# A four-layer graph network on one core: edge destinations loaded one round further ahead, and degree products made in one bf16 pass

## The reference, cut to what matters

```python
deg = segment_sum(ones_like(dst), dst, num_segments=n)                # degrees
x = layernorm(x + gcn(x, W1, b1, W2, b2, edge_index))                 # 2 sums over neighbours
x = layernorm(x + gated(x, src, dst, ...))                            # 1 sum (in and out)
agg = segment_sum(edge_attr_64, dst, num_segments=n)                  # edge attributes
x = layernorm(x + mlp(concat([x, agg, u]), w1, w2, w3))
x = layernorm(x + sage(x, src, dst, ...))                             # 2 sums over neighbours
```

## Time and profile before

| | |
|---|---|
| runs of the kernel before | 833.84, 836.97 and 837.99 us, median 836.97 |
| the profiled execution's own time | 836.0 us |
| its span, first to last instruction | 834.3 us |
| PE, DVE, ACT busy, share of the span | 88%, 70%, 40% |
| rounds of the first part | from 26 us to 230 us |
| mean granted clock of TensorE | 0.934 of full speed |

### The profile page before, as it was taken

One profiled execution on the slowest core, in us unless ns is written; L12 is line 12 of the kernel. 1 busy time (PEld: TensorE's weight loads), 2 busy tenths in 40 slices (PEclk: granted clock), 3 DMA queues, 4 the chain that ended last, 5 costly groups with the idle time before them and its releaser, 6 DMA issues.

```text
span 834.3 us, 20354 instructions
## 1 busy us (share of the span) xinstructions
PE 731.2 (88%) x8590; PEld 651.4 (78%) x8590; DVE 586.0 (70%) x884; ACT 329.8 (40%) x587; POOL 25.5 (3%) x44
## 2 busy tenths in 40 slices
PE   5467878888869999999989998869979999999994
PEld 2367868887769999899989996535539998699994
DVE  6999999989847777787876773757566554045554
ACT  0464545554544322522463223264325232432233
POOL 4700000000000000000000000000000000000000
PEclk9788997987969999999989999989988999999997
DMA  5445766766422000000000000000000000000001
GB/s 137 115 127 158 209 189 187 202 183 184 127 38 58 1 1 1 2 1 1 1 22 1 1 1 3 1 13 1 0 1 26 0 0 1 0 1 1 1 25 53
DMA packets 48710, 43.28 MB, mean 52 GB/s; under 512 B 26370, under 2 KB 31141, under 8 KB 48549
## 3 DMA queue, kind: packets, MB, share of 16 engines
q1 hardware_dynamic: 36042, 39.81, 17.0%
q10 hardware_dynamic: 11932, 0.81, 1.0%
q0 software_dynamic: 640, 1.29, 0.6%
HBM read 39.08 MB, written 2.01 MB: 49 GB/s over the span
## 4 chain that ended last, share of the span: by engine, by line
PE 76%; DVE 13%; issue 6%; ACT 2%; DMA 1%; SPq 1%; ACTq 0%; DVEq 0%
PE bank L1781 21%; PE bank L1782 21%; PE bank L1693 5%; PE bank L1709 4%; PE bank L1697 3%; PE bank L1678 2%; PE bank L1989 2%; PE bank L1713 2%; PE bank L1997 2%; PE bank L1843 1%; DVE early L1101 1%; PE bank L2040 1%; PE bank L2041 1%; PE bank L1794 1%; PE bank L1856 1%
## 5 line engine op out<-in xcount | busy, mean ns | idle before, releaser
L1781 PE MATMUL bank<-stage,f_hi 125*128 125x392 f32 x1000 | 348.7, 349 | 2.2 <-issue 2.2
L1782 PE MATMUL bank<-stage,f_lo 125*128 125x392 f32 x1000 | 342.4, 342 | 0.0
L1181 DVE CAST stage<-counts 125x2352 fp32r<-125x2352 uint8 x120 | 164.3, 1380 | 80.4 <-PE bank L1782 80.2
L828 ACT ACTIVATE stage<-counts 125x1568 fp32r<-125x1568 uint8 x80 | 108.1, 1351 | 227.6 <-PE bank L1782 224.6
L1781 PEld LDWEIGHTS bank<-stage,f_hi 125*128 125x128 f32 x1000 | 189.9, 190 | 3.5 <-issue 2.4
L1782 PEld LDWEIGHTS bank<-stage,f_lo 125*128 125x128 f32 x1000 | 189.8, 190 | 0.6
L781 ACT ACTIVATE counts<-bank 125x500 uint8<-125x500 f32 (+1 forms) x157 | 81.6, 594 | 58.2 <-PE bank L1697 55.9
L1693 PE MATMUL bank<-early 128*128 128x125 bf16 x625 | 81.5, 250 | 25.6 <-issue 17.8
L1693 PEld LDWEIGHTS bank<-early 128*128 128x128 bf16 x625 | 71.6, 116 | 27.7 <-issue 27.7
L1101 DVE TENSOR_TENSOR early<-tmp 128x5000 bf16<-128x5000 bf16 (+1 forms) x32 | 86.3, 2696 | 0.0
L1697 PE MATMUL bank<-early 128*128 128x75 bf16 x625 | 80.9, 225 | 0.5 <-issue 0.5
(11 more groups left out here) (244 smaller groups left out, 822.2 us busy)
## 6 DMA issues: line engine op xcount, KB each, us to landing
wb<-in_edge_attr SPq DMA_DIRECT2D x95, 256.0 KB, 3.2
rowb<-in_edge_attr SPq DMA_DIRECT2D x30, 256.0 KB, 3.3
wa<-in_x SPq DMA_DIRECT2D x12, 125.0 KB
out<-wl SPq DMA_DIRECT2D x6, 250.0 KB
tmp<-in_dst SPq DMA_DIRECT2D x63, 4.0 KB, 3.0
tmp<-in_dst ACTq DMA_DIRECT2D x62, 4.0 KB, 2.8
eaT<-eaT SPq DMA_DIRECT2D x1, 784.0 KB, 5.8
wb<-in_L_gnn_w_ih SPq DMA_DIRECT2D x1, 384.0 KB, 3.5
```

Source lines behind the costliest of these rows:

```text
L828: nc.scalar.activation(set_buffer(u, m), counts[:, SETS[u][0]:sum(SETS[u]), chunk(c)], ACT.Copy).then_inc(s["set_a_ready"], 1)
L1181: nc.vector.tensor_copy(set_buffer(u, m), counts[:, SETS[u][0]:sum(SETS[u]), chunk(pair * 2 + off)]).then_inc(s["set_d_ready"], 1)
L1781: mm(bank[h][:, 0:CH], f_hi[:, first + k, :], rhs[:, k, :], start=(first + k == 0), stop=False)
L1782: last = mm(bank[h][:, 0:CH], f_lo[:, first + k, :], rhs[:, k, :], start=False, stop=(first + k == HI - 1))
```

## The change

Destinations get a ring of `RD = 12` slots, three rounds, with three semaphores instead of two. SP issues the destinations of even block e + 4 where it issued those of block e, behind the same wait for block e - 8; ACT issues the odd ones of three rounds ahead instead of two, and six instead of four before the first round. For that SP loads a second start into a register, once for each even block. DVE's wait counts three semaphores; nothing else changes on DVE.

The degree products take bf16 operands: as weights the upper 16 bits of each fp32 element of the one-hot (`upper[r][:, :, 1]`, exact for 0 and 1), a step of two bf16 elements, and a bf16 one (`one_bf`) instead of the fp32 one. The number of matmuls in the program stays 8 for each edge block.

```diff
@@ -50,6 +50,7 @@
 ECAP = TE * 128
 EB = 4
 RE = 2 * EB
+RD = 3 * EB
 EPP = E // LO
 GE = 33
 NG = E // GE
@@ -171,7 +172,7 @@
 
         iota_l = carve(128).bitcast(BF16).rearrange("p (l j) -> p l j", j=2)
         iota_w = wl1[:, 400:400 + EB * TE * EW].rearrange("p (j w) -> p j w", w=EW)
-        dst_e = carve(RE * TE).bitcast(I32).rearrange("p (r j) -> p r j", r=RE)
+        dst_e = carve(RD * TE).bitcast(I32).rearrange("p (r j) -> p r j", r=RD)
         starts_i = carve(NE + 1)[0:1, :].bitcast(I32)
         key_base = carve(NQ)
         past_block = carve(NQ)
@@ -179,7 +180,8 @@
         oh_last = carve(3 * 2 * HI).bitcast(BF16).rearrange("p (b m k j) -> p b m k j", m=2, k=HI, j=2)
         crowded = carve(NQ)
         list_idx = carve(NQ).bitcast(I32)
-        one_f = wb[:, 6 * TE * DE:6 * TE * DE + 1]
+        one_bf = wb[:, 6 * TE * DE:6 * TE * DE + 1].bitcast(BF16)[:, 0:1]
+        upper = [a[:, :].bitcast(BF16).rearrange("p (w h) -> p w h", h=2) for a in oh_dst_row]
         ea_in = [a[:, r * TE * DE:(r + 1) * TE * DE].rearrange("p (j f) -> p j f", j=TE)
                  for a, n in ((wb, 6), (rowb[:, 2 * nd:], RE - 6)) for r in range(n)]
 
@@ -246,7 +248,7 @@
         g_rows_in = {k: sem(f"g_rows_in{k}") for k in (0, 1, 2, 3, 5, 6, 7)}
         out_done = [sem(f"out_done{b}") for b in range(3)]
         list_in = [sem(f"list_in{q}") for q in range(NQ)]
-        dst_ready = [sem(f"dst_ready{r}") for r in range(2)]
+        dst_ready = [sem(f"dst_ready{r}") for r in range(3)]
         ea_ready = [sem(f"ea_ready{r}") for r in range(2)]
 
         def wait_stored(eng, k):
@@ -564,15 +566,21 @@
             sp.wait_ge(s["starts_made"], 1)
             sp.wait_ge(s["slots_clean"], 1)
 
-            for e in range(NE):
+            def destinations(e):
+
                 if e == QL // BW + 1:
                     sp.wait_ge(s["starts_made"], 2)
+                sp.dma_start(dst_e[:, e % RD, :], dst[bass.ds(sp.value_load(starts_i[0:1, e:e + 1]), ECAP)].rearrange("(p j) -> p j", j=TE)).then_inc(dst_ready[e // EB % 3], 16)
+
+            for e in range(0, EB, 2):
+                destinations(e)
+            for e in range(NE):
                 first = sp.value_load(starts_i[0:1, e:e + 1])
                 if e >= RE:
                     sp.wait_ge(s["ea_made"], e - RE + 1)
                 sp.dma_start(ea_in[e % RE], edge_attr[bass.ds(first, ECAP), :].rearrange("(p j) c -> p j c", j=TE)).then_inc(ea_ready[e // EB % 2], 16)
-                if e % 2 == 0:
-                    sp.dma_start(dst_e[:, e % RE, :], dst[bass.ds(first, ECAP)].rearrange("(p j) -> p j", j=TE)).then_inc(dst_ready[e // EB % 2], 16)
+                if e % 2 == 0 and e + EB < NE:
+                    destinations(e + EB)
                 if e >= X_FROM and (e - X_FROM) % X_EVERY == 0 and (e - X_FROM) // X_EVERY <= PAIRS:
                     h = (e - X_FROM) // X_EVERY * 2
                     a, n = h * LO, min(2, HI - h)
@@ -670,7 +678,7 @@
                                     pattern=[[0, 1]], channel_multiplier=-1)
             for r in range(2):
                 nc.gpsimd.memset(oh_dst_row[r][:, nh:nd], 0.0)
-            nc.gpsimd.memset(one_f, 1.0).then_inc(s["slots_clean"], 1)
+            nc.gpsimd.memset(one_bf, 1.0).then_inc(s["slots_clean"], 1)
 
             for q in range(NQ):
                 pool.wait_ge(s["idx_made"], q + 1)
@@ -751,7 +759,7 @@
                 if e == QL // BW + 1:
                     act.wait_ge(s["starts_made"], 2)
                 first = act.value_load(starts_i[0:1, e:e + 1])
-                act.dma_start(dst_e[:, e % RE, :], dst[bass.ds(first, ECAP)].rearrange("(p j) -> p j", j=TE)).then_inc(dst_ready[e // EB % 2], 16)
+                act.dma_start(dst_e[:, e % RD, :], dst[bass.ds(first, ECAP)].rearrange("(p j) -> p j", j=TE)).then_inc(dst_ready[e // EB % 3], 16)
 
             def keep_apart(g):
 
@@ -768,7 +776,7 @@
                 nc.scalar.activation(eaT[0:DE + 1, EB * g * EW:(EB * g + ne) * EW], bank[5 + g % 2][0:DE + 1, FOLDED_AT:FOLDED_AT + ne * EW], ACT.Copy).then_inc(s["ea_kept"], 1)
 
             act.wait_ge(s["starts_made"], 1)
-            for e in range(1, RE, 2):
+            for e in range(1, RD, 2):
                 odd_list(e)
             keep_lists(0)
             act.wait_ge(s["pad_made"], 1)
@@ -785,7 +793,7 @@
                 keep_apart(g)
                 if g:
                     keep_edges(g - 1)
-                for e in range(EB * g + RE + 1, min(EB * g + RE + EB, NE), 2):
+                for e in range(EB * g + RD + 1, min(EB * g + RD + EB, NE), 2):
                     odd_list(e)
             keep_edges(NGP - 1)
 
@@ -1132,10 +1140,10 @@
 
                 es = edge_blocks(g)
                 ne = len(es)
-                dve.wait_ge(dst_ready[r], 16 * edges_of_side(g))
+                dve.wait_ge(dst_ready[g % 3], 16 * sum(len(edge_blocks(i)) for i in range(g % 3, g + 1, 3)))
                 if g >= 2:
                     dve.wait_ge(s["ea_made"], EB * (g - 1))
-                r0 = es[0] % RE
+                r0 = es[0] % RD
                 nc.vector.scalar_tensor_tensor(oh_dst[r][:, 0:ne * TE, :],
                                                dst_e[:, r0:r0 + ne, :].rearrange("p e (j a) -> p (e j) a", a=1).to_broadcast([128, ne * TE, EW]), -float(EB * g * EW),
                                                iota_w[:, 0:ne * TE, :],
@@ -1710,7 +1718,7 @@
                     for j in range(TE):
                         quad = 32 * (j % 4)
                         at = (k * TE + j) * EW
-                        last = mm(bank[5 + r][quad:quad + 32, k * (DE + 1) + DE:(k + 1) * (DE + 1)], oh_dst_row[r][:, at:at + 32], one_f, start=(j < 4), stop=(j >= 4))
+                        last = mm(bank[5 + r][quad:quad + 32, k * (DE + 1) + DE:(k + 1) * (DE + 1)], upper[r][:, at:at + 32, 1], one_bf, start=(j < 4), stop=(j >= 4))
                     last.then_inc(s["ea_made"], 1)
                 if g:
                     fold_quads(g - 1)
```

## The result

| | before | changed |
|---|---|---|
| median of 5 runs each | 836.20 us (833.45 to 837.99) | 828.79 us (827.84 to 829.22) |
| the profiled execution's span | 834.3 us | 827.6 us |
| PE, DVE, ACT busy | 88%, 70%, 40% | 86%, 71%, 40% |

The ratio is 0.9913, with a 95% interval of 0.9884 to 0.9941: 7.4 us faster. The prediction said 830.0 us in a range of 827.0 to 836.0.

A forecast was written before the change was run, and what follows sets the result against it. The rounds were taken as paced by DVE plus its waits for destinations, with PE nearly as full. -7.4 (destinations) +0.7 (lag) -0.3 (last edge blocks) = -7.0 us: profiled 836.0 to 829.0, median 830.0 us, range 827.0 to 836.0.

The forecast's parts named there:

- Destinations a round earlier: In the rounds, asking for destinations 5.73 us earlier removes DVE's seven waits at L1139: -7.4 us.
- 8.2 us of slack: PE's waits before a round's first product over 23 rounds, set against the 7.4 us that DVE can gain.
- the wait only moves: Rival: PE's 14.7 us of stalls stay, and DVE waits for PE or PE ends late; about 835.5 us, chance 0.13.
- This half of the edit is worth about nothing: Degree products on PE in the rounds: -5.5 us for halved passes against +6.4 us for mixed types.
- term for mixed types: Changing from bf16 to fp32 products after each block's degrees costs PE 0.07 us, +6.4 us for 92 blocks.
- the sign of "free": First degree pass to next block's first attribute pass: 0.06 us if changing type is free, 0.13 if 0.07 holds.
- Fewer instructions: -1.3: 18% fewer PE instructions a round shrink the 14.7 us of stalls by 2.7 us or nothing; half taken.
- The end of the rounds, +0.7 and -0.3: PE's lag at the rounds' end adds 0.7 us, between 0 and 2.0; round 30's four shorter edge blocks give -0.3.
- SP's second register load: nothing, but the cover is thin: 46 more loads give SP 13.8 us more work, leaving it short by 2.5 us over 23 rounds; taken as 0.
- ACT and the start of the program: nothing: Two more ACT loads of destinations before the first lists, and SP's two before its first attribute load, cost nothing.
- changes of type that drain the array: Rival: each block on PE pays 0.24 us for two type changes, gets 0.06 back; 845 to 846 us, chance 0.06.
- the floor of about 25 ns from start to start: Rival: by this floor, 736 PE passes left out free 18.4 us in the rounds; 829.3 us, chance 0.03.

The follow-up runs named there:

- the one pass: Kernel before the change with only the degree products made bf16 in one pass, destinations still in the ring of eight: 829.93 us, ratio 0.9939; again 829.80, ratio 0.9929.
- ring-only kernel: Changed kernel with the degree products back in fp32 (two passes), destinations still in the ring of twelve: 836.86 us, ratio 1.0004.
- the empty instructions: Changed kernel with 16 empty PE instructions, each with a semaphore increment, behind each edge block: 1087.34 us.

## Why the prediction was right, and where it was wrong

The total was right, 7.0 us predicted and 7.4 measured, and so was the pace after: DVE full, 5.73 us a round, the second part 7.0 us earlier. The reasons were not: the gain was put on the wrong half of the change.

- **"Destinations a round earlier: -7.4 us. All 7.4 us are on DVE's path": the step that failed.** It is worth 0 alone (1.0004) and about 1 to 2 us on top of the one pass. DVE's idle time had been read as a gain waiting to be had. In the ring-only kernel it is gone and DVE waits for PE instead, because PE could not go faster: it had 5.72 us of work and stalls a round against DVE's 5.73 before, and took 6.09 in the 14 rounds in which it waited for no comparison. The prediction had the number, 8.2 us of slack against a gain of 7.4, and counted on using it to the last. The slack of single rounds can't be used up so: a stall of 2.9 us in one round isn't covered by slack in another once the ring between them is full, which the ring-only timeline shows (5.4 us behind). The rival "the wait only moves", at 0.13, is what happens if this half is made alone. What pays is PE's relief, which either eight fewer fp32 passes (829.46) or eight bf16 ones in place of 16 fp32 (829.80) give without any ring.
- **"This half of the edit is worth about nothing": wrong by its two open terms.** The passes were right, 0.12 to 0.06 us a block, -5.5 us. The term for mixed types, +6.4 us, is 0: the text named 0.06 us as the sign of "free", and 0.06 it is. The 0.07 us taken from the earlier trace rows are real, but have another reason at that place than the type; a price read where two things change at once was put down to one of them.
- **"Fewer instructions: -1.3" between 0 and -2.7:** 9.3 us were measured, from 14.7 to 5.4, and 18% fewer instructions took 63% of the stalls. The bound was wrong because it assumed that stalls shrink in proportion. These are single executions: the others with PE as light left 4.7 to 8.1 us.
- **The clock was left out of the sum.** It rose from 0.85 to 0.91 in the rounds, worth about 7.2 us of PE's busy time. With passes, stalls and clock PE's slack became 24.6 us instead of 1.2, so nothing of SP's shortage was felt.
- **The end of the rounds, +0.7 and -0.3:** met in size in the one profiled execution. DVE's L1139 of round 30 came 7.7 us earlier (222.69 to 215.02). The counts of that round then ran at a granted clock of 0.53 and took 3.3 us up to the first edge block instead of 2.0 at 1.00, a lag of 1.3 for another reason than a late PE; its four edge blocks took 0.7 less, with a stall of 0.3 gone. Together that is the 7.0 us by which the second part starts earlier.
- **"SP's second register load: nothing, but the cover is thin": right for the time.** SP's waits went from 18.7 to 3.6 us, where a shortage of 2.5 had been reckoned, and PE waited 2.3 us for attributes where none were foreseen. One load more costs 10.8 us. **ACT and the start of the program: nothing, right.**
- The rivals: changes of type that drain the array have fallen (0.06 us). So has the floor of about 25 ns from start to start that the Trainium skill gives (TensorE: Matmul & The Clock Gate, "Wait — 56ns, not 53.3ns?"), as far as it is one for all products: 8 passes of one column take 0.06 us between the blocks, 7.5 ns each, as before. They take turns on four column groups, so that by these figures one group gets a pass every 30 ns, and within a group the runs here say nothing against the floor. The 829.3 us that went with it lies close to the result by chance, since its reason, much more slack on PE, was met in another way.

**What the stalls are.** The Trainium skill (Runtime: NRT & Kernel Launch, "Instruction fetch mechanics") holds that the fetching of instructions is hidden. The traces here do not agree. The stall of 2.93 us in the earlier trace rows ended at 124.85; between 122.5 and 123.6 us the instruction queue moved this one packet of 16 KB:

```profile
q8 instruction: 1, 0.02, 5.5%
```

It was done at 123.53, 1.3 us before PE went on. That is the rule: of the 108 stalls of over 0.25 us inside groups in the rounds' stretch of all traces but that of the empty instructions (thirteen, the repeated runs included), 105 end 1.2 to 1.6 us after a packet of that queue was done, though a packet comes only every 4 to 5.5 us. So a stall is PE waiting for its next instructions. The stalls also follow the number of PE's instructions, 10.1 to 22.0 us in the five kernels with 71 packets in the program and 4.7 to 8.1 in those with 63, and its pace, since none is left where empty instructions slow PE down. An estimate says why the edge blocks matter: a block is 64 instructions in 0.37 us, so that a packet of 256 would last PE 1.5 us there, while a packet takes about 1.0 us itself and 1.2 to 1.6 more until PE goes on. Why a packet is not asked for earlier, and how much of the gain is fetching and how much the passes themselves, stays open: passes and instructions were never parted. Also open is how the 24 us of PE's relief would divide if the clock had stayed.

## What to carry to other kernels

When two engines that feed each other through a ring of two rounds are both full to within 1% (5.72 and 5.73 us here), a wait on one of them is not yet a gain: ask what it would wait for next, and test each half of a change alone, because a correct total can rest on the wrong half. Late data behind a semaphore of a consumer may in part report that the consumer is late: here freeing PE removed 6.0 of DVE's 7.4 us of waits for a DMA. And an engine that only issues loads has a balance too: SP went from 18.7 us of waits to 3.6 by one 0.27 us load per two blocks, and one more would have cost 10.8. Last, count instructions where an engine's pieces are short: here 18% fewer of them on PE went with 9.3 of 14.7 us of stalls, and the packets of its own instructions told when it went on.

## What the runs showed that was not expected

- Changing between fp32 and bf16 products at each edge block costs nothing that shows: 0.06 us for 8 one-column passes up to the next block's first fp32 pass, and the same time for 8 fp32 passes (829.46) as for 8 bf16 ones (829.80).
- Small one-column passes on four column groups cost little by themselves (7.5 ns), but leaving out 1000 of them with their weight loads, spread over the rounds, took 9.3 us of stalls away and went together with the granted clock's step from 0.85 to 0.91. The step does not belong to the passes alone: with all 2000 of them the clock was 0.90 and 0.92 where the attributes' traffic was halved.
- An empty instruction with a semaphore increment costs PE 0.12 to 0.15 us, at least sixteen times the 7.5 ns of a one-column pass.
- PE stands still for up to 3.1 us in the middle of a group and goes on 1.2 to 1.6 us after a packet of its instructions was done, in 105 of 108 stalls.
- Halving the attributes' traffic (DMA share 0.70 to 0.44) ends all waits for destinations but leaves 12.0 of 14.7 us of PE's stalls.
